# An image phase without GpSimd: identity folded into the mixing weights, y and its sum in two VectorE steps, a third edge tap on TensorE, one deform tap on ScalarE

## What is computed

```python
m = jax.image.resize(mask, (B, 1, H, W), method='bilinear')
fuse = softmax(q k^T) v                                      # layer 0
hybrid = conv1x1(concat([x, fuse]), Wf, bf)
y = hybrid * m + x * (1 - m)

edge = relu(bn(dwconv3x3(y, edge_w)))                        # layer 1
att = sigmoid(relu(mean(y, (2, 3)) @ fc1_w.T) @ fc2_w.T)
o1 = bn1(conv1x1(concat([y * att, edge]), fusion_w, fusion_b))
out = bn2(conv1x1(dwconv3x3(o1, deform_w), balance_w, balance_b)) * y
```

## Time and profile before

| | us |
|---|---|
| median of three executions | 4298.28 |
| lowest, highest | 4297.22, 4299.57 |
| the profiled execution, its own time | 4293.3 |
| its span, first to last instruction | 4291.3 |

### The profile page before, as it was taken

How to read it: one execution, slowest core, us unless ns; L and a number is a source line. 1 busy time by engine, 2 the same in 40 slices (tenths; PEclk the granted TensorE clock), 3 DMA queues, 4 the chain that set the end, 5 groups by cost and what they waited for, 6 DMA issues and landing times. The chain is left out here.

```text
span 4291.3 us, 82398 instructions
## 1 busy us (share of the span) xinstructions
PE 4042.1 (94%) x20277; PEld 1972.5 (46%) x20277; DVE 3617.7 (84%) x5250; ACT 2450.8 (57%) x4584; POOL 3536.1 (82%) x1552
## 2 busy tenths in 40 slices
PE   7979999999999999999999999999999999877766
PEld 4534444444444444444444444444444444333322
DVE  3379999999899999998999999999999999377988
ACT  1216666666566666665666666666666666524344
POOL 3439999999889999998899999999999999846566
PEclk9959999999999999999999999999999999988888
DMA  6931100110011001100110011001100000030201
GB/s 194 284 85 39 40 20 21 41 40 20 20 41 40 20 21 41 40 20 21 41 40 20 21 41 40 20 21 41 40 20 21 21 20 17 7 94 15 74 20 39
DMA packets 213798, 184.92 MB, mean 43 GB/s; under 512 B 115986, under 2 KB 140740, under 8 KB 213316
## 3 DMA queue, kind: packets, MB, share of 16 engines
q1 hardware_dynamic: 213508, 181.74, 15.8%
HBM read 122.10 MB, written 59.24 MB: 42 GB/s over the span
## 5 line engine op out<-in xcount | busy, mean ns | idle before, releaser
L759 ACT ACTIVATE prob<-st 128x512 f32<-128x512 f32 x4096 | 2154.3, 602 | 1307.3 <-PE st L624 1049.1
L817 DVE TENSOR_REDUCE block_max<-mx 128x1 f32<-128x512 f32 x4096 | 2562.8, 683 | 340.7 <-PE mx L631 327.3
L488 POOL TENSOR_TENSOR prob_sum<-prob_sum,prob 128x1024 f32<-128x1024 f32 x768 | 1928.8, 2511 | 126.9 <-POOL prob_sum L488 95.3
L631 PE MATMUL mx<-keys,max_queries 96*128 96x512 f32 x4096 | 1647.9, 426 | 38.0 <-DMA keys<-k_scratch 27.6
L624 PE MATMUL st<-queries,keys 97*128 97x512 f32 x4096 | 1576.2, 411 | 1.4 <-ACT prob L759 1.3
L488 POOL TENSOR_TENSOR prob_sum<-prob 128x1024 f32<-128x1024 f32 x448 | 1066.8, 2381 | 251.9 <-ACT prob L759 251.9
L631 PEld LDWEIGHTS mx<-keys,max_queries 96*128 96x128 f32 x4096 | 778.4, 191 | 733.3 <-DVE block_max L817 562.5
L643 PE MATMUL acc<-prob,values 128*32 128x512 f32 x8192 | 1038.7, 602 | 0.0
L624 PEld LDWEIGHTS st<-queries,keys 97*128 97x128 f32 x4096 | 777.8, 190 | 520.7 <-ACT prob L759 283.6
L1200 POOL TENSOR_TENSOR conv<-conv,weighted_pixels 128x512 f32<-128x512 f32 x192 | 315.4, 1674 | 204.9 <-DVE conv L1258 121.3
L643 PEld LDWEIGHTS acc<-prob,values 128*32 128x32 f32 x8192 | 194.6, 109 | 426.9 <-issue 226.4
(11 more groups left out here) (122 smaller groups left out, 1426.9 us busy)
## 6 DMA issues: line engine op xcount, KB each, us to landing
max_queries<-q_scratch SPq DMA_DIRECT2D x384, 64.0 KB, 1.9
queries<-q_scratch SPq DMA_DIRECT2D x384, 64.0 KB, 1.9
keys<-k_scratch SPq DMA_DIRECT2D x168, 128.0 KB, 2.5
x<-in_x SPq DMA_DIRECT2D x18, 512.0 KB, 4.2
q_scratch<-high SPq DMA_DIRECT2D x32, 256.0 KB, 4.2
k_scratch<-high SPq DMA_DIRECT2D x16, 512.0 KB, 4.9
q_scratch<-low SPq DMA_DIRECT2D x32, 256.0 KB, 5.0
k_scratch<-low SPq DMA_DIRECT2D x16, 512.0 KB, 5.0
```

The lines of the kernel that those rows point to most:

```text
L488: ops.tensor_tensor(psum[k][:, :, :], a[:, :, :], prob[(first + i) % RING][:, :, :], ALU.add).then_inc(added[own], 1)
L631: nc.tensor.matmul(mx[bank(j, p)][:, :], qm[p][:, h, ns * P:(ns + 1) * P], kk[gp][0:SPLIT, h, blk * CH:(blk + 1) * CH], start=True, stop=T ...
L759: nc.scalar.activation(prob[s % RING][:, h, :], st[bank(i, p)][:, :], ACT.Exp).then_inc(exp_done, 1)
L817: nc.vector.tensor_reduce(bmax[p][:, j // MB, j % MB:j % MB + 1], mx[bank(j, p)][:, :], AX.X, ALU.max).then_inc(mx_taken, 1)
```

## The change

- The identity is subtracted once from the x half of the mixing weights (L1288 of the changed kernel, two steps of 128x128). The product then holds the mixed value less x, and VectorE needs no separate subtraction: it adds the bias and multiplies by the mask in one step (L1184), then adds x and sums in one step with an accumulating output (L1190). Four steps per tile become two.
- Edge taps: three on TensorE instead of two (`EDGE_PE`), six on VectorE instead of four, none on ScalarE and GpSimd.
- Deform taps: the first on ScalarE, straight into `conv` (`first_tap`, L1126), eight on VectorE instead of six, none on GpSimd. `first_tap` takes the place of `weigh_o1` in ScalarE's order and waits for the balance product that frees `conv[p]`.
- GpSimd keeps only the zeroing of the borders.
- The weights of the projection are released after that phase instead of being kept to the end, which makes room in SBUF; the buffers of later phases move to other addresses.

```diff
-EDGE_PE = 2
-SHARED = 3
-EDGE_DVE = TAPS - EDGE_PE - SHARED
-DEFORM_DVE = TAPS - SHARED
-ADDED = SHARED * CT
+EDGE_PE = 3
+EDGE_DVE = TAPS - EDGE_PE
+DEFORM_DVE = TAPS - 1
...
-                pe.wait_ge(diffed, freed(n))
+                pe.wait_ge(masked, freed(n))
...
-                pe.wait_ge(tap_added, added_in(deform_round(b, c), ADDED - 1))
+                pe.wait_ge(deform_step, CT * DEFORM_DVE * (n + 1))
...
+            pe.wait_ge(mixer, CT)
             for p in range(2):
                 mix(0, p, p, 0)
...
             def relu(b, c, p):
 
                 for ct in range(CT):
-                    act.wait_ge(tap_added, added_in(edge_round(b, c), ADDED - CT + ct))
+                    act.wait_ge(edge_step, EDGE_DVE * (EARLIER + CT * (b * NCH + c)) + CT * (EDGE_DVE - 1) + ct + 1)
...
-            def weigh_o1(b, c, nxt=1):
-                act.wait_ge(o1_ready, tile_done(b * NCH + c + nxt, CT - 1))
-                weigh(o1, "dtaps", b, c, deform_round(b, c))
+            def first_tap(b, c, p, nxt=1):
+
+                n = b * NCH + c
+                act.wait_ge(o1_ready, tile_done(n + nxt, CT - 1))
+                act.wait_ge(bal_mm, freed(n))
+                for ct in range(CT):
+                    nc.scalar.activation(as_rows(conv[p][:, ct, :]), inner(o1, ct, c, k=0), ACT.Identity,
+                                         scale=keep["dtaps"][:, ct, 0:1]).then_inc(tap_ready, 1)
...
             def make_y(b, c, p):
 
                 n = b * NCH + c
+                dve.wait_ge(mstep, NM * b + NM)
                 for ot in range(CT):
                     dve.wait_ge(hybrid, CT * n + ot + 1)
                     dve.wait_ge(y_ready, tile_done(n - 1, ot))
                     nc.vector.scalar_tensor_tensor(
-                        out=diff[:, ot, :], in0=front[p][ot][:, :],
-                        scalar=keep["vec"][:, VEC.index("bf"), ot:ot + 1], in1=xf[p][:, ot, :],
-                        op0=ALU.add, op1=ALU.subtract).then_inc(diffed, 1)
+                        out=as_rows(diff[:, ot, :]), in0=as_rows(front[p][ot][:, :]),
+                        scalar=keep["vec"][:, VEC.index("bf"), ot:ot + 1], in1=mask[:, bass.ds(c * ROWS, ROWS), :],
+                        op0=ALU.add, op1=ALU.mult).then_inc(masked, 1)
                 for ot in range(CT):
-                    dve.wait_ge(diffed, tile_done(n, ot))
-                    dve.wait_ge(mstep, NM * b + NM)
-                    nc.vector.tensor_tensor(as_rows(diff[:, ot, :]), as_rows(diff[:, ot, :]),
-                                            mask[:, bass.ds(c * ROWS, ROWS), :], ALU.mult).then_inc(masked, 1)
-                for ot in range(CT):
-                    dve.wait_ge(masked, CT * n + ot + 1)
-                    nc.vector.tensor_tensor(inner(y, ot, c), as_rows(diff[:, ot, :]),
-                                            as_rows(xf[p][:, ot, :]), ALU.add).then_inc(y_ready, 1)
-                for ot in range(CT):
-                    dve.wait_ge(y_ready, tile_done(n, ot))
-                    nc.vector.tensor_reduce(ypart[:, ot, bass.ds(c, 1)], inner(y, ot, c), AX.XY,
-                                            ALU.add).then_inc(part_ready, 1)
+                    dve.wait_ge(masked, tile_done(n, ot))
+                    nc.vector.scalar_tensor_tensor(
+                        out=inner(y, ot, c), in0=as_rows(diff[:, ot, :]), scalar=1.0, in1=as_rows(xf[p][:, ot, :]),
+                        op0=ALU.mult, op1=ALU.add, accum_out=ypart[:, ot, bass.ds(c, 1)]).then_inc(y_ready, 1)
...
                 dve.wait_ge(o1_ready, tile_done(n + nxt, CT - 1))
-                dve.wait_ge(edge_ready, tile_done(b * NCH + NCH - 2 + p, CT - 1))
-                dve.wait_ge(bal_mm, freed(n))
                 base = CT * DEFORM_DVE * n
-                for k in range(DEFORM_DVE):
+                for i in range(DEFORM_DVE):
                     for ct in range(CT):
+                        if i == 0:
+                            dve.wait_ge(tap_ready, CT * n + ct + 1)
+                        else:
+                            dve.wait_ge(deform_step, base + CT * (i - 1) + ct + 1)
...
+            for t in range(CT):
+                own = keep["wf"][:, t, t * P:(t + 1) * P]
+                nc.vector.tensor_tensor(own, own, keep["ident"][:, :], ALU.subtract).then_inc(mixer, 1)
```

More of the change, by code:

```diff
@@ L1173, in _ @@
                 fused(b, 1, 1)
-                weigh_o1(b, 0)
+                first_tap(b, 0, 0)
                 fused(b, 2, 0)
-                weigh_o1(b, 1)
+                first_tap(b, 1, 1)
                 with act.Fori(0, HALF - 2) as c2:
@@ L1179, in _ @@
                         fused(b, c2 * 2 + p + 3, 1 - p)
-                        weigh_o1(b, c2 * 2 + p + 2)
+                        first_tap(b, c2 * 2 + p + 2, p)
                         balanced(b, c2 * 2 + p, p, c2)
                 fused(b, NCH - 1, 1)
-                weigh_o1(b, NCH - 2)
+                first_tap(b, NCH - 2, 0)
                 balanced(b, NCH - 4, 0, HALF - 2)
-                weigh_o1(b, NCH - 1, nxt=0)
+                first_tap(b, NCH - 1, 1, nxt=0)
                 for c in range(NCH - 3, NCH):
@@ L1190, in _ @@
         def _(pool):
[L1191 to L1201, removed]
-            pool.sem_inc(tap_added, ADDED)
             for t in (y, o1):
@@ L1206, in _ @@
                     nc.gpsimd.memset(edge_rows, 0.0).then_inc(borders, 1)
-            with pool.Fori(0, B) as b:
-                with pool.Fori(0, HALF) as c2:
-                    for p in range(2):
-                        c = c2 * 2 + p
-                        add_taps(edge_round(b, c), p, edge_step,
-                                 EARLIER * EDGE_DVE + CT * EDGE_DVE * (b * NCH + c) + CT * (EDGE_DVE - 1))
-                with pool.Fori(0, HALF) as c2:
-                    for p in range(2):
-                        c = c2 * 2 + p
-                        add_taps(deform_round(b, c), p, deform_step,
-                                 CT * DEFORM_DVE * (b * NCH + c) + CT * (DEFORM_DVE - 1))
         @block.vector
@@ L1283, in deform @@
                 dve.wait_ge(o1_ready, tile_done(n + nxt, CT - 1))
[L1284 to L1285 removed]
                 base = CT * DEFORM_DVE * n
[L1287 removed]
+                for i in range(DEFORM_DVE):
                     for ct in range(CT):
+                        if i == 0:
+                            dve.wait_ge(tap_ready, CT * n + ct + 1)
+                        else:
+                            dve.wait_ge(deform_step, base + CT * (i - 1) + ct + 1)
                         dst = as_rows(conv[p][:, ct, :])
[L1290 to L1298 removed]
+                        nc.vector.scalar_tensor_tensor(out=dst, in0=inner(o1, ct, c, k=i + 1),
+                                                       scalar=keep["dtaps"][:, ct, i + 1:i + 2], in1=dst,
+                                                       op0=ALU.mult, op1=ALU.add).then_inc(deform_step, 1)
             def result(b, c, p):
@@ L1366, in build @@
         for w, ots, kts in WEIGHTS:
-            keep[w] = sb(f"{w}T", [P, kts, ots * P])
+            if w not in PROJECTIONS:
+                keep[w] = sb(f"{w}T", [P, kts, ots * P])
         scratch = {
@@ L1379, in build @@
         }
-        setup_phase(nc, dram, keep)
-        project_phase(nc, dram, keep, scratch)
+        with ExitStack() as first:
+            weights = {w: first.enter_context(nc.sbuf_tensor(f"{w}T", [P, kts, ots * P], F32))
+                       for w, ots, kts in WEIGHTS if w in PROJECTIONS}
+            setup_phase(nc, dram, {**keep, **weights})
+            project_phase(nc, dram, {**keep, **weights}, scratch)
         attention_phase(nc, keep, scratch)
```

29 lines of the change are left out of this document (5 added, 24 removed).

## The result

The changed kernel takes **4203.73 us** (median of 4 runs, 4202.27 to 4207.77), against 4298.48 (4297.22 to 4299.57) for the kernel before beside it. The ratio is **0.9784, 95% interval 0.9771 to 0.9797**. Its profiled execution took 4203.13 us with a span of 4201.3, against 4293.3 and 4291.3 before.

A forecast was written before the change was run, and what follows sets the result against it. VectorE was taken to bound the image phase, slowed by GpSimd's additions. Gains of 1.1 + 20.0 + 20.8 + 16.5 + 19.4 + 5.6 + 10.6 = 94 us take 4293.3 to 4199, plus 5.0 for the median: 4204, range 4195 to 4220.

The forecast's parts named there:

- its own case: Whole kernel: the forecast median of 4204 us with its small bounds; chance 0.72.
- The price of a step: Edge and deform stages: a VectorE step on 512 columns takes 0.663 us with GpSimd idle, first source PSUM or SBUF.
- rival B: Slow VectorE steps come with ScalarE and TensorE reading the same tiles, not GpSimd; 4388 us, slower than before; chance 0.04.
- The edge stage changes hands to TensorE: Edge stage: TensorE's 14 products set 12.04 us a chunk instead of 14.42; VectorE's 16 steps need 10.6.
- The unknown price: Edge stage: step writing y and its sum, absent from the trace, taken as 0.66 us; 1.26 or 1.68 considered.
- Rival A: Edge stage: the accumulating step is slow, 1.26 us or more; 4208 us, or 4217 at 1.68; chance 0.17.
- Step 4: Deform stage: ScalarE's queue keeps VectorE fed, about 3.8 us to spare; a store 4 us slower would surface.
- rival C: Store wait or input loads surface and VectorE waits; 4 us in each of 8 steady chunks, 4236 us; chance 0.05.
- Step 6: Tail after the last deform stage: GpSimd's last six additions go, 18.2 us becomes 7.6, gain 10.6.
- step 3: Deform stages: first image 112.4 to 95.9 us, upsampling unchanged at 16.8, gain 16.5; second image gain 19.4.
- step 5: Turn between the images: 30.7 to 25.1 us, including about 1 for loads or last's store, gain 5.6.

The follow-up runs named there:

- spare_adds: Changed kernel with GpSimd again doing six additions of 128x512 a chunk in both stages, on tiles nobody else uses: 4338.03 us, ratio 1.0098.
- sum_apart: Changed kernel with the step that writes y and its sum cut into a plain step and a separate reduction: 4200.73 us, ratio 0.9778.
- split13: Changed kernel with two instead of three edge taps of the second channel tile on TensorE: 4198.19 us, ratio 0.9774.
- fold_only: Kernel before with only the new two-step y and folded identity; GpSimd's additions, ScalarE's weighted copies and tap split stay: 4263.14 us, ratio 0.9925.

## Why the prediction was right

The forecast was 4204 us with 0.72 on its own case, in a range of 4195 to 4220; 4203.7 was measured. Its path was also right nearly throughout.

- **The price of a step, 0.663 us with GpSimd idle**: 42.49 us for 64 deform steps is 0.663. This carried the sum. `spare_adds` shows the reason given for it, not only the number, and rival B fell with it.
- **The edge stage changes hands to TensorE at 12.04 us**: 12.02, without gaps. `sum_apart` and `split13` show the change of hands by load on either side.
- **The unknown price**: the step that writes y with its sum was put at 0.66 and measured 0.61, against 0.60 for the same step without its sum (`sum_apart`). Rival A fell; the rule by which it would have cost 1.2 us (the Trainium skill, "Vector Engine (DVE) Microarchitecture Reference", section "Points that are easy to get wrong") is not borne out here, for the accumulating form as little as for the plain one.
- **Step 4, whether ScalarE keeps up**: the forecast left 3.8 us. The first tap is ready at 3937.7 (3936.35 + 1.33) and used at 3942.01, 4.3 us later. In the later chunks ScalarE waits for the store (9.6 us the longest inside the stage), and VectorE does not notice. So rival C fell as well, but for the load at the turn (below).
- **Step 6, the tail**: 7.9 us against 7.6.

Two terms of the sum were mis-sized, and cancelled. **"The second mask's upsampling unchanged at 16.8"** (step 3) measured 13.4: its two steps on 128x992 elements take 1.19 instead of 2.14 us, two small copies 0.20 instead of 1.14 and 1.19. They had met GpSimd too, as in `fold_only` and `spare_adds`, where the large ones take 2.14 again. Before and after:

```profile
4000.30 2.14 DVE L191 SCALAR_TENSOR_TENSOR m<-m,q 128x992 f32<-128x992 f32 x1
...
3966.34 1.19 DVE L193 SCALAR_TENSOR_TENSOR m<-m,q 128x992 f32<-128x992 f32 x1
```

The argument of the earlier trace rows should have been carried to every VectorE instruction of the stage: +3.5 us of gain.

**"About 1 for the loads or last's store"** (step 5) measured 4.5: 3.0 for the load, which the forecast's own 6 us from y to landing would have given as 2 (y at 10.6 + 2.5 us into the turn, the balance done at 17.3), and 1.5 for a mixing below full clock. These 3.5 us are the gain that the turn missed, but for 0.1.

That the two errors cancelled is luck, and so in part is that 4204 was met within 0.3 us. The phases ahead of the change took 4.0 us more in this execution, within the spread of the first mixing over all kernels (3764.0 to 3773.7), and the profiled execution after stands only 0.6 us below its median, where the forecast had added 5.0.

## What to carry to other kernels

Before giving GpSimd a share of the work, look at what VectorE does beside it: where VectorE bounds and its steps read two SBUF tiles, each GpSimd instruction that reads SBUF at the same time costs VectorE up to 1.0 us here (1.67 against 0.66 us a step of 512 columns). Price such a step from a row where GpSimd stands still, apply the difference to all of VectorE's instructions of the stage, and then ask which engine becomes the bound. Small orders at a turn between stages are worth working out with the load's latency, and measured against a time that leaves out the scatter of the phases before.

## What the runs showed of the hardware that was not expected

- The contention is not shared evenly. VectorE's two-source steps back to back starve GpSimd's reads: one addition of a single column took 36.73 us, one of 512 columns 34.54. Once GpSimd had got in, both alternated, at 1.67 us a VectorE step.
- GpSimd's fills leave VectorE's two-source steps at 0.66 us but can hold up its scalings and copies: two steps on 256 columns took 4.80 instead of 0.62 us, a copy of 32 columns 2.23 instead of 0.20. A scaling on 1984 columns was not held up (2.22 us with and without).
- Summing a result while it is written costs next to nothing: 0.61 us from step to step, against 0.60 for the same step without the sum, and 0.08 for the read-out, which lies under the next step.
